# Squares of the hidden layer folded to one tile by VectorE before TensorE sums them, and the last unit's sums after its down products

## Chip, cores, metric

One Trainium2 chip, one of its cores. The metric is the device time of one execution in microseconds (us); a comparison is made between runs of the two kernels on the same chip. The kernel before takes 1067.99 us, the median of three runs (1066.66 to 1070.09).

## What is computed

A transformer block over 16 batches of 256 tokens, width 256, in fp32: an attention part with 16 heads of 128, and a feed-forward part whose weights are first made ternary by groups of 64. The change touches the feed-forward part and its normalisation alone:

```python
h = jax.nn.silu(gate) * up                                   # hidden, 1024 wide
inv = jax.lax.rsqrt(jnp.mean(h * h, axis=-1, keepdims=True) + eps)
y = jnp.einsum('bsh,dh->bsd', h * inv, wq_p)                 # down product
x = x + _layernorm(y, axis=-1)
```

The kernel does not scale `h` by `inv`. A layernorm follows, so it takes the down product of the plain `h` (called z), and puts the mean of the squares into the layernorm's epsilon: z_floor = sum(h*h) * 1e-5/1024 + 1e-5*eps, one number a token. So the row sums of `h*h` are needed when z is normalised, not earlier.

## The kernel before, in words

Two phases follow each other, the attention over 128 steps and then the feed-forward over 16 **units** u, one a batch; the first units' work begins while the last attention steps drain. Everything of a unit lies in SBUF. Its hidden layer of 1024 x 256 tokens is held turned, as 8 tiles of 128 x 256, and worked in 4 **chunks** c of two tiles (FC = 2), so one VectorE or ScalarE instruction handles 128x512.

Every engine runs its own instruction list, written out by hand in its `step(u0, s)`; only semaphores tie them. `FLAG` says how many steps behind a stage stands: statistics and turn of the input two and one units ahead of the up products, the sums, down product and z one step behind them. Per unit:

- TensorE (`step`, L1021): `up` 0, `up` 1 of unit u (16 matmuls a chunk, `xt_hi`/`xt_lo` are the halves of the input), `down` of unit u-1 (L1000, 32 matmuls into `Z_BANK`), the sums of unit u-1 (`sum_tiles`, L990: a matmul with a column of ones for each token tile and each of the tiles given to it), `up` 2, `turn_x2` of unit u+1, `up` 3.
- ScalarE (`step`, from L1274): `norm_z` (L1262), then `activate` c (silu, L1231), `high_hidden` c (the fp32r high half of h, L1238), `norm_x2` (L1254), `square_hidden` c (L1245) and `split_x2` (L1271); the last square of a unit is its last instruction in a step but for what follows in the next step.
- VectorE (`step`, from L1669): `multiply` c (L1608: silu times up, one operand from PSUM), `add_squares` 2 and `sum_squares` of the unit before (L1615, L1621), `stats_x2` (L1628, L1631), `stats_z` with `sum_floor` (L1655, L1637, L1660), `split_x2` (L1665), `add_squares` 0 (L1615).
- GpSimd (`step`, from L689): `split_hidden` c (the low half of h, L644), `invert_x2` (from L651), `add_x` (the residual, L677), `invert_z` (from L665).

The squares of a unit are 8 tiles. Before, `add_squares` 0 adds tiles 2, 3 to 0, 1; `add_squares` 2 adds 6, 7 to 4, 5; `sum_squares` adds 4, 5 to 0, 1; two tiles remain, and TensorE sums them with 2 x 2 matmuls. For the last unit only `add_squares` 0 is done, and TensorE sums the six other tiles with 2 x 6 matmuls, ahead of its last down chunk.

A name in the trace is that of the memory it lies in: `wo_hi`, `wo_lo` are the halves of h (the attention's weights are no longer needed), `wq_hi`, `wq_lo` the up and down weights, `arena` holds the hidden layer, its squares and all small vectors. A fp32 matmul with `ones` leaves two records in the trace.

Of the kernel before, what the change touches and what calls it, by code (L numbers as in the profile page):

```python
# [25 lines left out]
ALU = mybir.AluOpType  # L26
AX = mybir.AxisListType

P = 128
# [40 lines left out]
FC = 2  # L70
# [13 lines left out]
def sandwich_kernel(nc, x, wq, wkv, wkvh, wg, wout, wgu, wproj, rope, out):  # L84
    ctx = ExitStack()
    with ctx:
# [3 lines left out]
        def sem(name):  # L90
            return ctx.enter_context(nc.semaphore(name))
# [38 lines left out]
        def carve(*shape):  # L130
# [154 lines left out]
                                     "lo_done"))  # L285
        gate_ready, up_ready, gate_silu, h_ready, h_squared, ht_hi_done, ht_lo_done = (
            sem(k) for k in ("gate_ready", "up_ready", "gate_silu", "h_ready", "h_squared", "ht_hi_done", "ht_lo_done"))
        h_added, h_summed, sum_ready, z_floored, z_ready = (
            sem(k) for k in ("h_added", "h_summed", "sum_ready", "z_floored", "z_ready"))
        z_stats, z_aggr, z_eps, z_neg, z_inv, z_biased, z_norm, res_done = (  # L290
            sem(k) for k in ("z_stats", "z_aggr", "z_eps", "z_neg", "z_inv", "z_biased", "z_norm", "res_done"))
        tile_done = sem("tile_done")
# [4 lines left out]
        def at_least(eng, s, value):  # L297

            if not (isinstance(value, int) and value <= 0):
                eng.wait_ge(s, value)  # L300
# [58 lines left out]
        def last_unit(u):  # L359

            return isinstance(u, int) and u == BATCH - 1
# [388 lines left out]
        def _(pe):  # L750
# [238 lines left out]
                                                   x2_rows(u, i)[:, t, k * P:(k + 1) * P], ident[:, :])  # L989
                last.then_inc(x2_turned, 1)  # L990

            def sum_tiles(u, i, tiles):

                at_least(pe, z_floored, u)
                for t in range(NT):
                    for f in tiles:
                        last = nc.tensor.matmul(O_BANK[:, t:t + 1], squares[i][:, f, t * P:(t + 1) * P], ones[:, :],  # L997
                                                start=t == 0 and f == 0, stop=f == tiles[-1], skip_group_check=True)
                last.then_inc(sum_ready, 1)

            def down(u, i):

                for c in range(FT // FC):
                    if last_unit(u) and c == FT // FC - 1:
                        pe.wait_ge(h_added, u * 2 + 1)
                        pe.wait_ge(h_squared, (u + 1) * (FT // FC))
                        sum_tiles(u, i, [*range(FC), *range(2 * FC, FT)])
                    pe.wait_ge(ht_lo_done, u * (FT // FC) + (c + 1))
                    if c == 0:
                        if isinstance(u, int) and u == 1:  # L1010
                            pe.wait_ge(y_copied, STEPS)
                        at_least(pe, z_norm, (u - 1) * NT)
                    for t in range(NT):
                        parts = [(f, part[i]) for f in range(c * FC, (c + 1) * FC) for part in (ht_hi, ht_lo)]
                        for n, (f, part) in enumerate(parts):

                            last = nc.tensor.matmul(Z_BANK[i][:, t * E:(t + 1) * E], part[:, f, t * P:(t + 1) * P],  # L1017
                                                    wpr_t[:, f, :], start=c == 0 and t == 0 and n == 0, stop=f == FT - 1,
                                                    skip_group_check=True)
                last.then_inc(z_ready, 1)  # L1020

            def step(u0, s):
                at = unit_at(u0, s, FLAG["up"])
                if at and at[0] > 0:
                    up(*at, 0)
                at = unit_at(u0, s, FLAG["up"])
                if at:
                    up(*at, 1)
                at = unit_at(u0, s, FLAG["down"])
                if at:  # L1030
                    u, i = at
                    down(u, i)
                    if not last_unit(u):
                        pe.wait_ge(h_summed, u + 1)
                        sum_tiles(u, i, range(FC))
                at = unit_at(u0, s, FLAG["up"])
                if at:
                    up(*at, 2)
                at = unit_at(u0, s, FLAG["turn"])
                if at and at[0] > 0:  # L1040
                    turn_x2(*at)
                at = unit_at(u0, s, FLAG["up"])
                if at:
                    up(*at, 3)
# [320 lines left out]
        def _(dve):  # L1365
# [251 lines left out]
            def sum_squares(u, i):  # L1617

                a, b = (squares[i][:, k * FC:(k + 1) * FC, :] for k in (0, 2))
                dve.wait_ge(h_added, u * 2 + 2)  # L1620
                nc.vector.tensor_tensor(a, a, b, ALU.add).then_inc(h_summed, 1)  # L1621

            def stats_x2(u):
# [9 lines left out]
            def sum_floor(u, i):  # L1633

                dve.wait_ge(sum_ready, u + 1)
                at_least(dve, z_eps, u - 1)
                nc.vector.tensor_scalar(z_floor[i], O_BANK[:, 0:NT], LN_EPS / FF, LN_EPS * RMS_EPS, ALU.mult, ALU.add)\  # L1637
                    .then_inc(z_floored, 1)
# [8 lines left out]

            def stats_z(u, i):

                if last_unit(u):  # L1650
                    sum_floor(u, i)
                dve.wait_ge(z_ready, u + 1)
                at_least(dve, z_biased, u)
                for t in range(NT):
                    nc.vector.bn_stats(z_stat[:, t, :], Z_BANK[i][:, t * E:(t + 1) * E]).then_inc(z_stats, 1)  # L1655
                if not last_unit(u):
                    sum_floor(u, i)
                dve.wait_ge(z_stats, u * NT + NT)
                for t in range(NT):
                    nc.vector.bn_aggr(z_agg[:, t, :], z_stat[:, t, :]).then_inc(z_aggr, 2)  # L1660

            def split_x2(u, i):

# [3 lines left out]
                    .then_inc(x2_lo_done, 1)  # L1667

            def step(u0, s):  # L1669
                at = unit_at(u0, s, FLAG["up"])  # L1670
                if at and at[0] > 0:
                    multiply(*at, 0)
                at = unit_at(u0, s, FLAG["out"])
                if at and last_unit(at[0]):
                    for t in range(NT):
                        add_x(*at, t)
                at = unit_at(u0, s, FLAG["sum"])
                if at and not last_unit(at[0]):
                    add_squares(*at, 2)
                    sum_squares(*at)  # L1680
                at = unit_at(u0, s, FLAG["stats"])
                if at and at[0] > 0:
                    stats_x2(at[0])
                at = unit_at(u0, s, FLAG["up"])
                if at:
                    multiply(*at, 1)
                at = unit_at(u0, s, FLAG["z"])
                if at:
                    stats_z(*at)
                at = unit_at(u0, s, FLAG["up"])  # L1690
                if at:
                    multiply(*at, 2)
                at = unit_at(u0, s, FLAG["turn"])
                if at and at[0] > 0:
                    split_x2(*at)
                at = unit_at(u0, s, FLAG["up"])
                if at:
                    add_squares(*at, 0)
                    multiply(*at, 3)
# [136 lines left out]
```

## Time and profile before

| | |
|---|---|
| median of three runs | 1067.99 us |
| the profiled execution, its own time | 1069.97 us |
| span of its trace | 1068.2 us |
| TensorE busy | 1045.1 us (98%) |
| GpSimd busy | 932.6 us (87%) |
| ScalarE busy | 861.3 us (81%) |
| VectorE busy | 812.7 us (76%) |
| granted TensorE clock | 0.993 of full |
| feed-forward phase | about 856 us to the end |

The time of an execution is its span and some 2 us around it. Busy time is that of the records; matmuls overlap, so a busy TensorE isn't one at its peak. Each row of a timeline has a start and a duration in us, then engine, line, operation, tiles (out<-in), and in brackets the idle time before it with what ended that.

### The profile page before, as it was taken

The numbers are of one execution on the slowest core, as the hardware profiler recorded it, in microseconds if no ns is written. First come the engines' busy times: TensorE is split into PE (matmuls) and PEld (weight loads), VectorE is DVE, ScalarE is ACT, GpSimd is POOL, SyncE is SP. The second block draws the span as 40 slices with busy tenths as digits, with TensorE's granted clock in tenths as the row PEclk, the third lists the DMA queues.
The fourth block names the chain that finished last, engine by engine and source line by source line (L and its number), as shares of the span: only waits on it lengthen the run. The fifth ranks groups of instructions, "written<-read, shape, count | busy, mean of one in ns | idle before, by whom it ended". The sixth has DMA issues, their size and how long they took to land.

```text
span 1068.2 us, 25271 instructions
## 1 busy us (share of the span) xinstructions
PE 1045.1 (98%) x7978; PEld 1002.8 (94%) x7978; DVE 812.7 (76%) x2804; ACT 861.3 (81%) x2386; POOL 932.6 (87%) x928
## 2 busy tenths in 40 slices
PE   7899999999999999999999999999999999999997
PEld 6789999999999999999999999999999899999997
DVE  5777888878887888888788878886777656666653
ACT  4788888888898889888988898888888766666674
POOL 4688999999999999999999999999899658777785
PEclk8999999999999999999999999999999999999999
DMA  8451111112111211221121121111120000000001
GB/s 264 173 169 31 51 55 54 45 50 61 41 41 56 66 41 32 62 69 41 48 64 42 40 61 51 50 41 62 51 90 21 2 1 21 21 21 20 22 21 41
DMA packets 35125, 58.58 MB, mean 55 GB/s; under 512 B 3136, under 2 KB 16000, under 8 KB 34688
## 3 DMA queue, kind: packets, MB, share of 16 engines
q1 hardware_dynamic: 34992, 56.96, 17.1%
q8 instruction: 64, 1.05, 0.4%
q14 instruction: 69, 0.57, 0.2%
HBM read 50.92 MB, written 9.18 MB: 56 GB/s over the span
## 4 chain that ended last, share of the span: by engine, by line
POOL 61%; PE 20%; issue 15%; DVE 1%; ACT 1%; DMA 1%; POOLq 1%; ACTq 0%; DVEq 0%
POOL arena L595 15%; POOL arena L616 14%; POOL arena L627 14%; POOL arena L605 13%; PE psum L975 11%; PE psum L1017 5%; PE psum L997 1%; POOL arena L553 1%; POOL arena L577 1%; PE psum L755 1%; POOL X L586 1%; PE psum L988 1%; DMA arena<-kh_rows 0%; POOL arena L561 0%; POOLq L300 0%
## 5 line engine op out<-in xcount | busy, mean ns | idle before, releaser
L627 POOL TENSOR_TENSOR arena<-arena 128x768 f32<-128x768 f32 x128 | 196.1, 1532 | 17.5 <-DVE arena L1503 17.2
L605 POOL TENSOR_TENSOR arena<-arena 128x512 f32<-128x512 f32 x128 | 173.7, 1357 | 10.0
L595 POOL TENSOR_TENSOR arena<-arena,tables 128x512 f32<-128x512 f32 x128 | 166.7, 1302 | 16.3 <-ACT arena L1167 14.8
L1516 DVE SCALAR_TENSOR_TENSOR pt_split<-psum,vh_col,pt_split 128x256 fp32r<-128x256 f32 (+1 forms) x512 | 176.9, 406 | 2.7 <-ACT pt_split L1197 2.7
L616 POOL TENSOR_TENSOR arena<-arena 128x512 f32<-128x512 f32 x128 | 164.0, 1281 | 3.7 <-ACT arena L1141 3.1
L887 PE MATMUL psum<-arena 128*128 128x256 f32 x512 | 154.6, 384 | 3.3 <-POOL arena L605 3.1
L1178 ACT ACTIVATE arena<-arena 128x256 f32<-128x256 f32 x256 | 128.4, 502 | 32.0 <-DVE arena L1493 25.6
L755 PE MATMUL psum<-wo_hi,o_hi 128*128 128x256 f32 x512 | 152.7, 298 | 0.0
L755 PE MATMUL psum<-xt_hi,wq_hi 128*128 128x256 f32 x512 | 146.8, 287 | 0.0
L755 PE MATMUL psum<-xt_lo,wq_hi 128*128 128x256 f32 x512 | 145.3, 284 | 0.0
L755 PE MATMUL psum<-xt_hi,wq_lo 128*128 128x256 f32 x512 | 145.2, 284 | 0.0
L755 PE MATMUL psum<-wo_hi,o_lo 128*128 128x256 f32 x512 | 144.3, 282 | 0.0
L755 PE MATMUL psum<-wo_lo,o_hi 128*128 128x256 f32 x512 | 143.7, 281 | 0.0
L755 PE MATMUL psum<-pt_split,vals_hi 128*128 128x512 f32 (+1 forms) x512 | 142.0, 358 | 1.1 <-DVE wo_lo L1377 0.8
L975 PE MATMUL psum<-xt_hi,wq_hi 128*128 128x256 f32 x512 | 128.4, 290 | 0.8 <-DVE xt_lo L1665 0.8
L975 PE MATMUL psum<-xt_lo,wq_hi 128*128 128x256 f32 x512 | 124.7, 281 | 0.0
L1196 ACT ACTIVATE pt_split<-psum,vh_col 128x256 fp32r<-128x256 f32 x256 | 120.9, 472 | 0.1
L1166 ACT ACTIVATE arena<-psum 64x512 f32<-64x512 f32 x128 | 76.1, 595 | 53.6 <-DVE arena L1478 53.3
L1525 DVE TENSOR_TENSOR o_lo<-psum,o_hi 128x512 fp32r<-128x512 f32 x128 | 87.3, 682 | 33.5 <-ACT o_hi L1206 31.7
L889 PEld LDWEIGHTS psum<-arena 128*128 128x128 f32 x512 | 98.0, 191 | 13.7
L644 POOL TENSOR_TENSOR wo_lo<-arena,wo_hi 128x512 fp32r<-128x512 f32 x64 | 88.8, 1396 | 22.9 <-ACT wo_hi L1238 22.7
L1491 DVE CUSTOM_DVE_ANT_0 arena<-psum,mask 128x256 f32<-128x256 f32 x256 | 106.9, 417 | 1.1 <-issue 1.1
(185 smaller groups left out, 3448.4 us busy)
## 6 DMA issues: line engine op xcount, KB each, us to landing
arena<-kh_rows SPq DMA_DIRECT2D x127, 256.0 KB, 3.3
out<-spare SPq DMA_DIRECT2D x15, 256.0 KB, 2.1
arena<-w_rows SPq DMA_DIRECT2D x6, 512.0 KB, 4.7
X<-L_attn_Wout SPq DMA_DIRECT2D x1, 2048.0 KB, 14.7
X<-L_attn_x SPq DMA_DIRECT2D x1, 2048.0 KB, 13.6
arena<-L_attn_Wq SPq DMA_DIRECT2D x1, 1536.0 KB, 10.4
X<-L_attn_x SPq DMA_DIRECT2D x1, 1536.0 KB, 10.5
w_rows<-L_ffn_w_gate_up SPq DMA_DIRECT2D x3, 512.0 KB, 9.0
```

What stands on the lines that cost most here:

```text
L595: nc.gpsimd.tensor_tensor(swap, swap, spread, ALU.mult).then_inc(q_sined, 1)
L605: nc.gpsimd.tensor_tensor(q_rot[p % 2], q_cos[p % 2], q_swap[p % 2], ALU.add).then_inc(q_roped, 1)
L616: nc.gpsimd.tensor_tensor(k_head[p % 2], keys[par].unsqueeze(1).to_broadcast([P, HP, N]), kh_all[p % 4], ALU.mult).then_inc(k_scaled, 1)
L627: nc.gpsimd.tensor_tensor(tb, tb, r.unsqueeze(3).to_broadcast([P, HP, 3, P]), ALU.mult).then_inc(p_ready, 1)
L755: last = nc.tensor.matmul(o, a, b, start=start and i == 0, stop=stop and i == len(passes) - 1, skip_group_check=skip)
L887: nc.tensor.matmul(sj[:, 0:2 * P], q[:, j, P:N], kt[:, j, :], start=True, stop=True, skip_group_check=True)
L889: nc.tensor.matmul(sj[:, 2 * P:3 * P], q[:, j, 0:P], kt[:, j, 0:P], start=False, stop=True, skip_group_check=True).then_inc(s_ready, 1)
L975: last = nc.tensor.matmul(bank[c % 2 * 2 + half][:, j * N:(j + 1) * N], wgu_t[:, k, col:col + P], part[:, k, :], start=n == 0 and j == 0, ...
L1178: nc.scalar.activation(tb[:, j, 0:2 * P], tb[:, j, 0:2 * P], ACT.Exp, scale=-1.0, bias=nmax[p % 4][:, 2 * j:2 * j + 1], accum_out=rsum[p % ...
L1196: nc.scalar.activation(pt_hi[p % 2][:, j * N:(j + 1) * N], b[:, 0:N], ACT.Copy, scale=vh[:, 0, h:h + 1])
L1491: nc.vector.tensor_tensor_reduce(tb[:, j, 0:2 * P], S_BANK[j][:, 0:2 * P], mask[:, :], -1.0, -MASKED, ALU.add, ALU.min, nmax[p % 4][:, 2 * ...
L1516: last = nc.vector.scalar_tensor_tensor(pt_lo[p % 2][:, o], b[:, i], vh[:, t, h:h + 1], pt_hi[p % 2][:, o].bitcast(F32), ALU.mult, ALU.sub ...
```

## The change

`sum_squares` gets a second instruction: after two tiles remain, one is added to the other (128x256), and it waits for the first by a new semaphore, `h_halved`. TensorE sums the one remaining tile, with two matmuls. The last unit is treated like the others: all three kinds of add on VectorE, and two matmuls after its whole down product. On VectorE `add_squares` 2 and `sum_squares` of the unit before now stand at the head of the step, ahead of `multiply` 0, and `sum_floor` stands behind the aggregates of `stats_z` (in the last unit it stood ahead of `stats_z`).

```diff
@@ -285,8 +285,8 @@
                                      "lo_done"))
         gate_ready, up_ready, gate_silu, h_ready, h_squared, ht_hi_done, ht_lo_done = (
             sem(k) for k in ("gate_ready", "up_ready", "gate_silu", "h_ready", "h_squared", "ht_hi_done", "ht_lo_done"))
-        h_added, h_summed, sum_ready, z_floored, z_ready = (
-            sem(k) for k in ("h_added", "h_summed", "sum_ready", "z_floored", "z_ready"))
+        h_added, h_halved, h_summed, sum_ready, z_floored, z_ready = (
+            sem(k) for k in ("h_added", "h_halved", "h_summed", "sum_ready", "z_floored", "z_ready"))
         z_stats, z_aggr, z_eps, z_neg, z_inv, z_biased, z_norm, res_done = (
             sem(k) for k in ("z_stats", "z_aggr", "z_eps", "z_neg", "z_inv", "z_biased", "z_norm", "res_done"))
         tile_done = sem("tile_done")
@@ -989,22 +989,18 @@
                                                    x2_rows(u, i)[:, t, k * P:(k + 1) * P], ident[:, :])
                 last.then_inc(x2_turned, 1)
 
-            def sum_tiles(u, i, tiles):
-
+            def sum_tiles(u, i):
+
+                pe.wait_ge(h_summed, u + 1)
                 at_least(pe, z_floored, u)
                 for t in range(NT):
-                    for f in tiles:
-                        last = nc.tensor.matmul(O_BANK[:, t:t + 1], squares[i][:, f, t * P:(t + 1) * P], ones[:, :],
-                                                start=t == 0 and f == 0, stop=f == tiles[-1], skip_group_check=True)
+                    last = nc.tensor.matmul(O_BANK[:, t:t + 1], squares[i][:, 0, t * P:(t + 1) * P], ones[:, :],
+                                            start=t == 0, stop=True, skip_group_check=True)
                 last.then_inc(sum_ready, 1)
 
             def down(u, i):
 
                 for c in range(FT // FC):
-                    if last_unit(u) and c == FT // FC - 1:
-                        pe.wait_ge(h_added, u * 2 + 1)
-                        pe.wait_ge(h_squared, (u + 1) * (FT // FC))
-                        sum_tiles(u, i, [*range(FC), *range(2 * FC, FT)])
                     pe.wait_ge(ht_lo_done, u * (FT // FC) + (c + 1))
                     if c == 0:
                         if isinstance(u, int) and u == 1:
@@ -1030,9 +1026,7 @@
                 if at:
                     u, i = at
                     down(u, i)
-                    if not last_unit(u):
-                        pe.wait_ge(h_summed, u + 1)
-                        sum_tiles(u, i, range(FC))
+                    sum_tiles(u, i)
                 at = unit_at(u0, s, FLAG["up"])
                 if at:
                     up(*at, 2)
@@ -1618,6 +1612,9 @@
 
                 a, b = (squares[i][:, k * FC:(k + 1) * FC, :] for k in (0, 2))
                 dve.wait_ge(h_added, u * 2 + 2)
+                nc.vector.tensor_tensor(a, a, b, ALU.add).then_inc(h_halved, 1)
+                a, b = (squares[i][:, k, :] for k in range(FC))
+                dve.wait_ge(h_halved, u + 1)
                 nc.vector.tensor_tensor(a, a, b, ALU.add).then_inc(h_summed, 1)
 
             def stats_x2(u):
@@ -1647,17 +1644,14 @@
 
             def stats_z(u, i):
 
-                if last_unit(u):
-                    sum_floor(u, i)
                 dve.wait_ge(z_ready, u + 1)
                 at_least(dve, z_biased, u)
                 for t in range(NT):
                     nc.vector.bn_stats(z_stat[:, t, :], Z_BANK[i][:, t * E:(t + 1) * E]).then_inc(z_stats, 1)
-                if not last_unit(u):
-                    sum_floor(u, i)
                 dve.wait_ge(z_stats, u * NT + NT)
                 for t in range(NT):
                     nc.vector.bn_aggr(z_agg[:, t, :], z_stat[:, t, :]).then_inc(z_aggr, 2)
+                sum_floor(u, i)
 
             def split_x2(u, i):
 
@@ -1667,6 +1661,10 @@
                     .then_inc(x2_lo_done, 1)
 
             def step(u0, s):
+                at = unit_at(u0, s, FLAG["sum"])
+                if at:
+                    add_squares(*at, 2)
+                    sum_squares(*at)
                 at = unit_at(u0, s, FLAG["up"])
                 if at and at[0] > 0:
                     multiply(*at, 0)
@@ -1674,10 +1672,6 @@
                 if at and last_unit(at[0]):
                     for t in range(NT):
                         add_x(*at, t)
-                at = unit_at(u0, s, FLAG["sum"])
-                if at and not last_unit(at[0]):
-                    add_squares(*at, 2)
-                    sum_squares(*at)
                 at = unit_at(u0, s, FLAG["stats"])
                 if at and at[0] > 0:
                     stats_x2(at[0])
```

On VectorE, in a steady step, the rows from a unit's first `add_squares` to the aggregates of its z. Before (L1615 add, L1608 multiply, L1621 `sum_squares`, L1628 and L1631 `stats_x2`, L1655 and L1660 `stats_z`, L1637 `sum_floor`; of the two L1608 the second is `multiply` 0 of the next unit):

```order
L1615 TENSOR_TENSOR arena<-arena 128x512
L1608 TENSOR_TENSOR arena<-arena,psum 128x512 x2
L1615 TENSOR_TENSOR arena<-arena 128x512
L1621 TENSOR_TENSOR arena<-arena 128x512
L1628 BN_STATS arena<-X 128x6 x2
L1631 BN_AGGR arena<-arena 128x2 x2
L1608 TENSOR_TENSOR arena<-arena,psum 128x512
L1655 BN_STATS arena<-psum 128x6 x2
L1637 TENSOR_SCALAR arena<-psum 128x2
L1660 BN_AGGR arena<-arena 128x2 x2
```

In the changed kernel (L1609 add, L1602 multiply, L1615 `sum_squares`, L1618 its new second add, L1625 and L1628 `stats_x2`, L1650 and L1653 `stats_z`, L1634 `sum_floor`):

```order
L1609 TENSOR_TENSOR arena<-arena 128x512
L1602 TENSOR_TENSOR arena<-arena,psum 128x512
L1609 TENSOR_TENSOR arena<-arena 128x512
L1615 TENSOR_TENSOR arena<-arena 128x512
L1618 TENSOR_TENSOR arena<-arena 128x256
L1602 TENSOR_TENSOR arena<-arena,psum 128x512
L1625 BN_STATS arena<-X 128x6 x2
L1628 BN_AGGR arena<-arena 128x2 x2
L1602 TENSOR_TENSOR arena<-arena,psum 128x512
L1650 BN_STATS arena<-psum 128x6 x2
L1653 BN_AGGR arena<-arena 128x2 x2
L1634 TENSOR_SCALAR arena<-psum 128x2
```

`multiply` 0 of the next unit moved from ahead of the second add to behind three adds, and `sum_floor` from between the z statistics to behind them.

On TensorE, around the last unit's sums (L1017, and L1013 in the changed kernel, are the down product, L997 the sums). Before, the sums and what stands on both sides of them:

```order
L1017 MATMUL psum<-wq_lo,wo_hi 128x256
L1017 MATMUL psum<-wq_lo,wo_lo 128x256
L997 MATMUL psum<-ones,arena 128x1 x12
L1017 MATMUL psum<-wq_lo,wo_hi 128x256
L1017 MATMUL psum<-wq_lo,wo_lo 128x256
```

In the changed kernel, the end of the list:

```order
L1013 MATMUL psum<-wq_lo,wo_hi 128x256
L1013 MATMUL psum<-wq_lo,wo_lo 128x256
L1013 MATMUL psum<-wq_lo,wo_hi 128x256
L1013 MATMUL psum<-wq_lo,wo_lo 128x256
L997 MATMUL psum<-ones,arena 128x1 x2
L86 UNCONDITIONAL_BRANCH
```

Twelve matmuls ahead of the last eight down products became two behind them.

## Rows read from the trace of the kernel before

**Rows 1.** the page, part 1: busy us and share of the span, instructions

```profile
PE 1045.1 (98%) x7978; PEld 1002.8 (94%) x7978; DVE 812.7 (76%) x2804; ACT 861.3 (81%) x2386; POOL 932.6 (87%) x928
```

**Rows 2.** chain that ended last, 1030 us to the end: start, us, what

```profile
1050.61 0.79 PE psum L997 x8
...
1058.21 2.59 PE psum L997 x24
...
1063.13 0.19 POOL arena L665
```

**Rows 3.** waits from 850 us on: who for whom, us in total, times, longest

```profile
PEld psum L975 <- DVE xt_lo L1665: 3.1, 12, 0.5
```

**Rows 4.** timeline of VectorE, 974 to 990 us: start, us, engine, line, operation

```profile
976.45 0.68 DVE L1665 TENSOR_TENSOR xt_lo<-psum,xt_hi 128x512 fp32r<-128x512 f32 x1
977.05 1.76 DVE L1615 TENSOR_TENSOR arena<-arena 128x512 f32<-128x512 f32 x1
978.73 0.67 DVE L1608 TENSOR_TENSOR arena<-arena,psum 128x512 f32<-128x512 f32 x1
982.02 0.69 DVE L1608 TENSOR_TENSOR arena<-arena,psum 128x512 f32<-128x512 f32 x1 [2.61 <-ACT arena L1231]
982.62 0.68 DVE L1615 TENSOR_TENSOR arena<-arena 128x512 f32<-128x512 f32 x1
983.34 0.69 DVE L1621 TENSOR_TENSOR arena<-arena 128x512 f32<-128x512 f32 x1
...
985.03 0.69 DVE L1608 TENSOR_TENSOR arena<-arena,psum 128x512 f32<-128x512 f32 x1
...
989.53 0.68 DVE L1665 TENSOR_TENSOR xt_lo<-psum,xt_hi 128x512 fp32r<-128x512 f32 x1
```

**Rows 5.** timeline of ScalarE, 974 to 990 us

```profile
979.98 0.61 ACT L1245 ACTIVATE arena<-arena 128x512 f32<-128x512 f32 x1
...
981.40 0.59 ACT L1231 ACTIVATE arena<-psum 128x512 f32<-128x512 f32 x1
982.74 0.63 ACT L1238 ACTIVATE wo_hi<-arena 128x512 fp32r<-128x512 f32 x1 [0.75 <-DVE arena L1608]
983.28 0.58 ACT L1231 ACTIVATE arena<-psum 128x512 f32<-128x512 f32 x1
...
986.28 1.08 ACT L1254 ACTIVATE arena<-X,arena 128x256 f32<-128x256 f32 x2
```

**Rows 6.** timeline of GpSimd, 974 to 990 us

```profile
976.98 1.28 POOL L677 TENSOR_TENSOR spare<-arena,X 128x512 f32<-128x512 f32 x1
978.22 0.64 POOL L665 TENSOR_TENSOR arena<-arena 128x2 f32<-128x2 f32 x1
...
979.95 2.55 POOL L644 TENSOR_TENSOR wo_lo<-arena,wo_hi 128x512 fp32r<-128x512 f32 x2
983.45 1.75 POOL L644 TENSOR_TENSOR wo_lo<-arena,wo_hi 128x512 fp32r<-128x512 f32 x1 [0.95 <-ACT wo_hi L1238]
```

**Rows 7.** timeline of VectorE, the end of the kernel

```profile
1060.82 0.16 DVE L1637 TENSOR_SCALAR arena<-psum 128x2 f32<-128x2 f32 x1 [4.70 <-PE psum L997]
...
1065.08 0.88 DVE L1645 TENSOR_TENSOR spare<-arena,X 128x256 f32<-128x256 f32 x2 [2.09 <-ACT arena L1262]
```

**Rows 8.** timeline of VectorE, 853 to 885 us

```profile
870.93 1.79 DVE L1615 TENSOR_TENSOR arena<-arena 128x512 f32<-128x512 f32 x1
872.65 0.67 DVE L1608 TENSOR_TENSOR arena<-arena,psum 128x512 f32<-128x512 f32 x1
876.42 0.69 DVE L1608 TENSOR_TENSOR arena<-arena,psum 128x512 f32<-128x512 f32 x1 [3.10 <-ACT arena L1231]
...
879.44 0.69 DVE L1608 TENSOR_TENSOR arena<-arena,psum 128x512 f32<-128x512 f32 x1
```

**Rows 9.** timeline of GpSimd, 853 to 885 us

```profile
870.89 1.29 POOL L644 TENSOR_TENSOR wo_lo<-arena,wo_hi 128x512 fp32r<-128x512 f32 x1 [0.64 <-ACT wo_hi L1238]
```

**Rows 10.** timeline of GpSimd, 1055 to 1059 us

```profile
1056.87 1.30 POOL L644 TENSOR_TENSOR wo_lo<-arena,wo_hi 128x512 fp32r<-128x512 f32 x1 [0.62 <-ACT wo_hi L1238]
```

## The prediction

> **What bounds the kernel now.** I read the page first. TensorE is busy for 1045.1 of 1068.2 us [rows 1], and each feed-forward unit gives it eight records of row sums, 0.79 us in the chain [rows 2]. That reading alone says: halve them and win. The second view is the waits from 850 us on. TensorE does wait there, for the low half of the next unit's input, 12 times for 3.1 us, 0.26 us each [rows 3]; so once a unit TensorE stands at the end of somebody else's chain. The third view, one steady step on VectorE, GpSimd and ScalarE, shows that chain closed into a ring:
>
> - VectorE's `split_x2` from 976.45, first `add_squares` from 977.05 (it takes 1.76 us), `multiply` 3 from 978.73 [rows 4];
> - ScalarE's last square, 979.98 to 980.59, then `norm_z`, `activate` 0 from 981.40 [rows 5];
> - `multiply` 0 from 982.02, second `add_squares`, `sum_squares`, `stats_x2`, `multiply` 1 from 985.03 [rows 4];
> - ScalarE's `norm_x2` of the next unit from 986.28, the squares and `activate` 2 behind it [rows 5], and VectorE's `split_x2` again at 989.53: 13.08 us after the first [rows 4].
>
> No link of the ring has slack, except that `activate` 1 is over at 983.86, 1.17 us before the `multiply` that reads it: VectorE is busy with adds and statistics. TensorE alone would need 13.08 - 0.26 = 12.8 us. What counts is therefore when `multiply` 1 runs.
>
> **The port, which sets the durations.** The first `add_squares` takes 1.76 us, the second, of the same shape, 0.68 [rows 4]. The first starts 0.07 us after GpSimd's `add_x` (976.98 to 978.26) and ends 0.55 us after it; GpSimd's next, tiny instruction takes 0.64 us [rows 6] where it takes 0.19 at the end of the kernel [rows 2]. The other way round, `split_hidden` 0 starts at 983.45 under `sum_squares`, takes 1.75 us in place of 1.28 and ends 1.17 us after VectorE's 984.03 [rows 4, 6]. So an add of two SBUF tensors and a GpSimd instruction exclude each other; the waiting one goes next, even where the other engine has more work queued. `multiply`, which reads one operand from PSUM, overlaps GpSimd from 982.02 at its usual 0.69. The Trainium skill (SBUF — State Buffer, "Who interferes with whom") says that a VectorE instruction with two SBUF inputs contends with a GpSimd one that reads SBUF, and the later blocks fully: by that rule the trace agrees, and it speaks against moving such adds under GpSimd's long instructions.
>
> **The change part by part.**
>
> 1. TensorE: two matmuls a unit go, half of the eight records of 0.79 us [rows 2]: -0.40 us of its work. Worth nothing while the ring is slower.
>
> 2. VectorE gets one add of 128x256. Its price: the final residual adds, 128x256 of two SBUF inputs, take 0.88 for two overlapped, some 0.42 each [rows 7]; the bounds are 0.16 (the small floor instruction in the same rows) and 0.69 (the 512-column form). I take 0.42, nearest in shape.
>
> 3. The order: all three adds now stand ahead of `multiply` 0, behind ScalarE's last square (980.59). VectorE was idle there, from 979.4 to 982.02. With the port free, the adds would run 980.65 to 982.4 and `multiply` 0 would be 0.3 us late, `multiply` 1 about 1 us early. But GpSimd runs `split_hidden` 2 and 3 back to back from 979.95 to 982.50 [rows 6]. Laid out with the two offsets above: `split_hidden` 2 ends 981.23, the second `add_squares` 981.23 + 0.55 = 981.78; GpSimd waits for it and ends `split_hidden` 3 at 981.78 + 1.17 = 982.95. `sum_squares` must wait for the add's semaphore, so GpSimd is next in line: the sum ends at 982.95 + 0.55 = 983.50, the new add at 983.96, `multiply` 0 starts about 983.88: **1.86 us late**.
>
> 4. What is queued behind it: on ScalarE `high_hidden` 0 starts 0.72 after `multiply` 0, `activate` 1 another 0.54, and takes 0.58 [rows 5]; with 0.07 of semaphore `multiply` 1 starts 1.91 us after `multiply` 0, at 985.79 in place of 985.03. The statistics (about 1.1 us) fit in between. **The ring becomes 0.76 us longer per unit**, and everything from `norm_x2` to the next `add_squares` keeps its relative place, the 0.07 us by which GpSimd's `add_x` is ahead too. Bounds: -0.24 (VectorE keeps the port, below) and +0.9 (if the sum and the new add each pay 0.07 more in handing over). `split_hidden` 0 gets out from under the sum, which saves GpSimd 0.45 us that nobody waits for. TensorE: the last down chunk starts near 983.8 and has its low half at 982.95; the sums need `h_summed` at 983.96, TensorE comes to them after 984.5. Both are covered by the down products; without that cover the sums would cost up to 0.4.
>
> 5. Moving `sum_floor` behind the aggregates puts 0.14 us later on a result that GpSimd takes up several us later: nothing.
>
> 6. Entry. In unit 1 the first `add_squares` (870.93) is held by `split_hidden` 2 [rows 8, 9], which started 0.04 us before. TensorE is the bound there, and is 0.40 us ahead after the first shorter sum, so the add starts near 870.5, ahead of `split_hidden` 2, and costs 0.7. `multiply` 3, then held by TensorE, comes at about 871.3 in place of 872.65. Only one `split_hidden` (about 872.75 to 874.05) stands in the way of the new adds: 874.6, 875.3, 875.75; `multiply` 0 at 875.7 (before 876.42), `multiply` 1 at 875.7 + 1.91 = 877.6 (before 879.44): -1.8 us. Bounds: -0.4 (TensorE's share alone) and -1.9.
>
> 7. The end. Twenty-four records of sums, 2.59 us, stood between unit 15's third and fourth down chunk [rows 2]. They go: the last chunk then starts when its low half is there; before, that was 1058.17 [rows 10], when TensorE had just begun the sums. The price is VectorE's three adds behind the last square and one `split_hidden`, about 0.5 us past the last down product, with `sum_floor` (0.16) at the end. So -2.6 from the sums; but only about 0.3 comes back, since the first add and most of its wait fall under the down products: -2.3. Bounds: 0 and -2.6.
>
> **The sum.** Twelve steps (`multiply` 1 of units 3 to 14) at +0.76 are +9.1; entry -1.8; end -2.3: **+5.0 us**. Against the profiled execution's 1069.97 us that is 1075.0; that execution lies 2 us over the median of the three runs, 1067.99, so I forecast **1073.0 us** for the median. A measurement of this kernel can tell about 0.3%, 3.2 us, from no change. The forecast's own range, 0.6 to 0.9 a step and 0 to -2.6 at the end, is 1070 to 1077.
>
> **The rivals.**
>
> *A: VectorE keeps the port between its dependent adds* (ends on the other side). The adds then end 981.78, 982.50 and 982.96, `multiply` 0 starts at 982.88, `multiply` 1 at 984.79, 0.24 us earlier than now. It decides if GpSimd's waiting instruction is not let in during the 0.04 us between an add and the next that waits for it (the gap between 983.30 and 983.34 in [rows 4]). Twelve times -0.24, -1.8 and -2.3 give -7.0: 1061. Against it: GpSimd leaves no longer gap between `add_x` and its next instruction, and VectorE got in. Chance 0.14.
>
> *B: the adds are not held up at all, TensorE is the bound.* The ring falls under TensorE's time, and a unit saves 0.26 + 0.40 us: 12 x 0.66 = 7.9, with 0.4 at entry and 2.3 at the end -10.6: 1057. Against it stands the 1.76 us add. For it: 98% busy on the page. Chance 0.07.
>
> *C: the places shift so that in half of the steps the first `add_squares` gets ahead of `add_x`.* It lost by 0.07 us [rows 4, 6]; ahead, it ends up to 1.1 us earlier. Half the steps at that gain are 12 x (0.76 - 0.55) = +2.5, so -1.6 in all: 1066.4. Both engines count from the same end of `norm_x2`, which speaks against a shift; for it there is only how small 0.07 us is. Chance 0.13.
>
> **How the numbers follow.** Forecast 0.66. Of it 0.05 falls under +3.2 us. Slower by over 0.3%: 0.61. Within: 0.05 + 0.12 of C = 0.17. Faster: A and B and the rest of C, 0.22. The range reaches from A's 1061 to the forecast's upper end 1077, and leaves out B and the tails, under 0.2.
>
> **What would show it.** In a steady step of the changed kernel: the second `add_squares` takes about 1.2 us, `sum_squares` 1.7, the new add 0.42; `split_hidden` 3 about 1.7; `multiply` 1 to `multiply` 1 is 13.8 us; TensorE waits about 1.3 us a unit, at the turn and for `split_x2`. At the end, the first down chunk to the last instruction is 2 us shorter. The forecast is wrong if `sum_squares` takes 0.69 us right behind the add (A), if no add is over 0.8 us (B), or if the first `add_squares` comes back to 0.7 (C). It would be wrong in size if `multiply` 0 started under 1.5 us later after the last square than I say, 3.3 us.

## The result, and the profile after

The changed kernel takes 1073.18 us, the median of 12 runs (1071.71 to 1076.28); the kernel before, measured beside it, 1068.08 us (12 runs, 1066.66 to 1070.52). The ratio is 1.0044 (95% interval 1.0034 to 1.0053): slower by 0.4%, clear of the spread, 5.1 us at the medians.

The page's first part, against [rows 1]: TensorE's busy time fell by 8.8 us and VectorE's rose by 27.2, although the work added to VectorE is 16 adds of 0.42 us and the last unit's two. Nearly all of the rest is time in which its adds stood still: an instruction that is held up has a longer record, not an idle time before it.

```profile
PE 1036.3 (97%) x7898; PEld 991.8 (93%) x7898; DVE 839.9 (78%) x2822; ACT 861.8 (81%) x2386; POOL 933.6 (87%) x928
```

A steady step on VectorE (start, us, engine, line, operation; the line numbers moved by 6: L1602 `multiply`, L1609 `add_squares`, L1615 `sum_squares`, L1618 the new add, L1659 `split_x2`):

```profile
977.00 0.68 DVE L1659 TENSOR_TENSOR xt_lo<-psum,xt_hi 128x512 fp32r<-128x512 f32 x1
977.60 1.75 DVE L1609 TENSOR_TENSOR arena<-arena 128x512 f32<-128x512 f32 x1
979.27 0.67 DVE L1602 TENSOR_TENSOR arena<-arena,psum 128x512 f32<-128x512 f32 x1
981.17 1.17 DVE L1609 TENSOR_TENSOR arena<-arena 128x512 f32<-128x512 f32 x1 [1.22 <-ACT arena L1239]
982.37 1.67 DVE L1615 TENSOR_TENSOR arena<-arena 128x512 f32<-128x512 f32 x1
984.07 0.42 DVE L1618 TENSOR_TENSOR arena<-arena 128x256 f32<-128x256 f32 x1
984.41 0.68 DVE L1602 TENSOR_TENSOR arena<-arena,psum 128x512 f32<-128x512 f32 x1
...
986.28 0.69 DVE L1602 TENSOR_TENSOR arena<-arena,psum 128x512 f32<-128x512 f32 x1 [0.17 <-ACT arena L1225]
...
990.77 0.68 DVE L1659 TENSOR_TENSOR xt_lo<-psum,xt_hi 128x512 fp32r<-128x512 f32 x1
```

and on GpSimd in the same step (L677 `add_x`, L644 `split_hidden`, the pair with 3.00 us being 2 and 3):

```profile
977.52 1.28 POOL L677 TENSOR_TENSOR spare<-arena,X 128x512 f32<-128x512 f32 x1
...
980.49 3.00 POOL L644 TENSOR_TENSOR wo_lo<-arena,wo_hi 128x512 fp32r<-128x512 f32 x2
985.84 1.29 POOL L644 TENSOR_TENSOR wo_lo<-arena,wo_hi 128x512 fp32r<-128x512 f32 x1 [2.35 <-ACT wo_hi L1232]
```

The second `add_squares` takes 1.17 us where [rows 4] have 0.68, `sum_squares` 1.67 where they have 0.69, and the pair of `split_hidden` 3.00 where [rows 6] have 2.55. `multiply` 0 starts 3.27 us after ScalarE's last square (which ends 981.14) where before it started 1.43 us after it (982.02 against 980.59): 1.84 us late. `multiply` 1 follows 1.87 us behind `multiply` 0. From `split_x2` to `split_x2` the step is 13.77 us, 0.69 longer than the 13.08 of [rows 4].

TensorE waits more. The waits between 930 and 1020 us, seven units, after:

```profile
PEld psum L988 <- ACT arena L1248: 6.0, 7, 0.9
PE psum L988 <- ACT arena L1248: 4.5, 7, 0.7
PEld psum L975 <- DVE xt_lo L1659: 3.4, 7, 0.5
PE psum L975 <- DVE xt_lo L1659: 1.9, 7, 0.3
```

That is 0.9 us a unit of idle matmul time (4.5 and 1.9 us in seven), 1.3 us for weight loads, where before the same window had 0.3 and 1.6 us in all.

**Where the 5 us are.** Each of the 16 units has one `split_x2`, and each has a row, so a profiled execution can be cut at them. I start at unit 1's; unit 0's lies 39.6 us ahead of it in both kernels, among the last attention steps. From unit 1's to the end of the span, the kernel before takes 211.3 us (856.87 to 1068.2) and the changed one 216.25 us (854.35 to 1070.6), 4.9 us more. The first two steps after that cut, 13.02 and 12.39 us where 13.46 and 13.60 stood, are the entry, 1.65 us gained. The next twelve, from unit 3's to unit 15's (879.76 to 1045.91), are 166.15 us against 157.76 (883.93 to 1041.69): 8.4 lost. The rest, 24.69 against 26.51, is the end: 1.8 gained.

The twelve are not all alike. Nine lost 0.68 to 0.74 us each. The first lost 0.42: its first `add_squares` took 1.47 us in the changed kernel and 1.74 before. One lost 0.38, because there the kernel before stood 0.33 us ahead of `multiply` 1 for a reason that the profile doesn't show. The last lost 1.21: it has no `stats_x2`, which made it the shortest before (12.59 us), but in the changed kernel it took 13.80 like the others.

### The profile page after: what moved, and what is told of

It is laid out like the page before. It is cut to its first block, busy times and chain, and to the rows that moved or that the text cites. A ratio compares the mean times of both kernels' runs of the same rounds, so it can differ in the third digit from the quotient of the medians.

```text
span 1070.6 us, 25129 instructions
## 1 busy us (share of the span) xinstructions
PE 1036.3 (97%) x7898; PEld 991.8 (93%) x7898; DVE 839.9 (78%) x2822; ACT 861.8 (81%) x2386; POOL 933.6 (87%) x928
## 4 chain that ended last, share of the span: by engine, by line
POOL 58%; issue 16%; PE 16%; DVE 5%; ACT 3%; DMA 1%; POOLq 0%; ACTq 0%; DVEq 0%
POOL arena L595 15%; POOL arena L616 14%; POOL arena L627 13%; POOL arena L605 12%; PE psum L975 8%; PE psum L1013 4%; PE psum L755 2%; DVE arena L1602 1%; ACT arena L1248 1%; POOL arena L553 1%; POOL arena L577 1%; PE psum L988 1%; DVE arena L1609 1%; ACT arena L1225 1%; POOL X L586 1%
## 5 line engine op out<-in xcount | busy, mean ns | idle before, releaser
L644 POOL TENSOR_TENSOR wo_lo<-arena,wo_hi 128x512 fp32r<-128x512 f32 x64 | 88.3, 1388 | 37.1 <-ACT wo_hi L1232 36.9
```

## Experiments

The theory: VectorE, ScalarE and GpSimd form a ring that is the bound of a step, and what lengthens it is that VectorE's adds of two SBUF tensors and GpSimd's instructions exclude each other. The rivals: the new add costs by its duration alone; the order costs nothing; TensorE is the bound. In the table, "step" is the usual distance of two `split_x2` between 930 and 1000 us, "last 12" the time from unit 3's `split_x2` to unit 15's, "end" from there to the end of the span. "Fold" is short for the new add of 128x256 with the two matmuls that it saves.

| kernel | ratio to before (95%) | median us | step | last 12 | end |
|---|---|---|---|---|---|
| before | 1 | 1068.1 to 1069.1 | 13.07 | 157.8 | 26.5 |
| changed | 1.0044 (1.0034 to 1.0053) | 1073.2 | 13.78 | 166.2 | 24.7 |
| changed, run again | 1.0045 (1.0028 to 1.0061) | 1073.5 | 13.78 | 166.1 | 24.7 |
| fold, old order | 1.0111 (1.0095 to 1.0127) | 1081.3 | 14.51 | 173.0 | 25.1 |
| new order, no fold | 0.9983 (0.9974 to 0.9993) | 1067.5 | 13.32 | 159.8 | 25.0 |
| last unit alone | 0.9987 (0.9977 to 0.9997) | 1067.2 | 13.08 | 157.9 | 25.2 |
| TensorE's matmuls given back | 1.0065 (1.0050 to 1.0081) | 1075.8 | 13.78 | 166.4 | 26.0 |
| reductions for the wide adds | 0.9998 (0.9987 to 1.0009) | 1068.3 | 13.47 | 162.0 | 24.2 |
| adds behind `multiply` 1, fold | 0.9899 (0.9879 to 0.9918) | 1056.8 | 12.34 | 149.2 | 25.7 |
| the same, no fold | 0.9936 (0.9919 to 0.9954) | 1062.9 | 12.79 | 153.5 | 25.2 |

**Fold in the old order.** The three adds go back behind `multiply` 0.

```diff
             def step(u0, s):
-                at = unit_at(u0, s, FLAG["sum"])
-                if at:
-                    add_squares(*at, 2)
-                    sum_squares(*at)
                 at = unit_at(u0, s, FLAG["up"])
                 if at and at[0] > 0:
                     multiply(*at, 0)
...
+                at = unit_at(u0, s, FLAG["sum"])
+                if at:
+                    add_squares(*at, 2)
+                    sum_squares(*at)
                 at = unit_at(u0, s, FLAG["stats"])
```

> The change with its three adds put back behind multiply 0 (the order before), fold and last unit kept. Theory (the port decides): split_hidden 0 of GpSimd starts under sum_squares and is next in line when that ends, so the new 0.42 us add waits for it and ends about 1.4 us after sum_squares; multiply 1 then starts about 1.4 us later than before in every steady step, the step is 14.4 us, the kernel 12 x 1.4 - 2 (end) - 1 (entry) = about +14 us, 1082. Rival (an add costs its 0.42 us, the port matters nowhere else than at the first add): +0.46 us a step, the kernel +2 to +3 us, 1070.5.

Measured: 1081.3 us, a step of 14.51. VectorE, then GpSimd:

```profile
989.45 0.69 DVE L1609 TENSOR_TENSOR arena<-arena 128x512 f32<-128x512 f32 x1
990.17 0.69 DVE L1615 TENSOR_TENSOR arena<-arena 128x512 f32<-128x512 f32 x1
990.90 1.40 DVE L1618 TENSOR_TENSOR arena<-arena 128x256 f32<-128x256 f32 x1
992.23 0.74 DVE L1625 BATCH_NORM_STATS2 arena<-X 128x6 f32<-128x256 f32 x2
```

```profile
990.28 1.74 POOL L644 TENSOR_TENSOR wo_lo<-arena,wo_hi 128x512 fp32r<-128x512 f32 x1 [0.94 <-ACT wo_hi L1232]
```

Neither wide add is held; the new one, of 256 columns, takes 1.40 us, because `split_hidden` 0 came at 990.28 under `sum_squares`, waited, and went in between the two dependent adds. This is the hand-over on which rival A rested, in a place of its own: GpSimd gets the port. Fold and last unit together, in the old order, cost 12.2 us against the kernel before. The right partner for the fold alone is the kernel "last unit alone" below, which differs from this one by the fold only: the fold costs 14.0 us at the medians, 1.43 us a step (14.51 against 13.08). The new order takes back half of that, 0.73 us a step.

**New order without the fold.** `sum_squares` ends with the wide add, and TensorE sums two tiles.

```diff
-                nc.vector.tensor_tensor(a, a, b, ALU.add).then_inc(h_halved, 1)
-                a, b = (squares[i][:, k, :] for k in range(FC))
-                dve.wait_ge(h_halved, u + 1)
                 nc.vector.tensor_tensor(a, a, b, ALU.add).then_inc(h_summed, 1)
```

> The new order without the new add: TensorE sums two tiles again (four matmuls a unit). Theory: without the 0.42 us add and its 0.04 of semaphore, multiply 0 comes 1.4 us late against before instead of 1.86, multiply 1 +0.30 us, a step 13.4 us; entry -1, end -2: about +0.6 us, 1068.7. Rival (the new add is the whole loss, the order costs nothing): a step of 12.9 us (TensorE's), the kernel 4 to 6 us faster than before.

Measured: 1067.5 us, a step of 13.32. The wide adds take 1.16 and 1.67 us as in the changed kernel. So the order alone costs 0.25 us a step, and the fold on top of it 0.46, its 0.42 us and a semaphore. The total came out better than expected, 1.8 us under the kernel before by the ratio where +0.6 was expected: over the last 12 steps the order cost 2.0 us, the expectation has 3.6.

**The last unit alone**, in the kernel before. In the last unit VectorE now does all three wide adds, as in the others, where it did only `add_squares` 0, and TensorE does four matmuls behind the down product in place of twelve inside it. `sum_floor` stands behind the aggregates, as in the changed kernel.

```diff
             def down(u, i):
...
-                    if last_unit(u) and c == FT // FC - 1:
-                        pe.wait_ge(h_added, u * 2 + 1)
-                        pe.wait_ge(h_squared, (u + 1) * (FT // FC))
-                        sum_tiles(u, i, [*range(FC), *range(2 * FC, FT)])
...
                     down(u, i)
-                    if not last_unit(u):
-                        pe.wait_ge(h_summed, u + 1)
-                        sum_tiles(u, i, range(FC))
+                    sum_tiles(u, i)
...
-                if at and not last_unit(at[0]):
+                if at:
                     add_squares(*at, 2)
                     sum_squares(*at)
```

> The kernel before, with its last unit alone handled like the others (three adds on VectorE, four matmuls behind the whole down product). Theory: steady steps unchanged at 13.07 us, the 2.59 us of sums go from the end and some 0.6 us come back by the wait for the squares' sum: 1.9 us faster, 1066.2. Rival (VectorE's adds and GpSimd's residual in the same port give it all back): no change.

Measured: 1067.2 us, a gain of 1.4 us by the ratio (0.3 to 2.5); in the profile the end is 1.35 us shorter (25.16 against 26.51), the steady step is as before (13.08) and the last 12 take 157.9 us against 157.8. The rival has part of it: at the end the adds are held here too (1.37 and 1.65 us, not 0.69 each), but that doesn't give it all back.

**TensorE's work given back** to the changed kernel.

```diff
                 for t in range(NT):
-                    last = nc.tensor.matmul(O_BANK[:, t:t + 1], squares[i][:, 0, t * P:(t + 1) * P], ones[:, :],
-                                            start=t == 0, stop=True, skip_group_check=True)
+                    for r in range(2):
+                        last = nc.tensor.matmul(O_BANK[:, t:t + 1], squares[i][:, 0, t * P:(t + 1) * P], ones[:, :],
+                                                start=t == 0 and r == 0, stop=r == 1, skip_group_check=True)
```

> The changed kernel with each of its two sum matmuls done twice, so TensorE has its 0.40 us a unit again (the row sums come out doubled). Theory (the ring of VectorE, ScalarE and GpSimd is the bound, TensorE waits 1.3 us a unit): no change against the changed kernel, 1073 (at most +0.2). Rival (TensorE is the bound, 97% busy): +0.40 us a unit, 1079.

Measured: 1.0065, against 1.0044 for the changed kernel; the intervals touch, the ratios are 2.2 us apart. Neither number was expected. The profile separates them: the step is 13.78 us, the same to 0.01, so in the steady part TensorE's 0.4 us are free; they are taken out of its wait at the turn, which falls from 4.5 to 1.4 us in the seven units above. But the first three steps are 0.45, 0.67 and 0.29 us longer than in the changed kernel, and the end 1.3 us: there TensorE's work counts, and the theory's "at most +0.2" had left both out. At the entry it counts twice, because with the matmuls back the first `add_squares` comes behind `split_hidden` 2 again and takes 1.80 us (at 867.16) in place of 0.68. The end on VectorE, `sum_floor` (L1635) waiting for the doubled sums:

```profile
1065.70 0.25 DVE L1654 BATCH_NORM_AGGREGATE arena<-arena 128x2 f32<-128x6 f32 x2
1066.63 0.16 DVE L1635 TENSOR_SCALAR arena<-psum 128x2 f32<-128x2 f32 x1 [0.67 <-PE psum L998]
```

**Reductions in place of the wide adds**, one SBUF input each.

```diff
-                nc.vector.tensor_tensor(a, a, b, ALU.add).then_inc(h_added, 1)
+                if c:
+                    dve.wait_ge(h_added, u * 2 + 1)
+                    nc.vector.tensor_reduce(squares[i][:, FC:2 * FC, :], pairs(squares[i][:, 2 * FC:4 * FC, :]), AX.X, ALU.add)\
+                        .then_inc(h_added, 1)
+                else:
+                    nc.vector.tensor_tensor(a, a, b, ALU.add).then_inc(h_added, 1)
...
-                nc.vector.tensor_tensor(a, a, b, ALU.add).then_inc(h_halved, 1)
+                nc.vector.tensor_reduce(squares[i][:, 2 * FC:3 * FC, :], pairs(squares[i][:, 0:2 * FC, :]), AX.X, ALU.add)\
+                    .then_inc(h_halved, 1)
```

> The changed kernel with its second add_squares and its sum_squares written as a pairwise tensor_reduce: one SBUF input each, twice the elements read, so about 1.2 us each where a free add takes 0.68. Theory (port): nothing holds them, nor do they hold split_hidden 3; 1.2 + 1.2 + 0.42 against 1.17 + 1.67 + 0.42, multiply 0 comes about 0.4 us earlier than in the changed kernel, a step 13.35 us, the kernel about 5 us faster than the changed one, 1068. Rival (the adds are slow for another reason, such as GpSimd's traffic in SBUF slowing every VectorE instruction, or the semaphores): the reductions take 1.7 us and more, the kernel is 6 us or more slower than the changed one.

Measured: 1068.3 us, a step of 13.47. VectorE, then GpSimd:

```profile
978.10 1.25 DVE L1615 TENSOR_REDUCE arena<-arena 128x512 f32<-128x1024 f32 x1 [1.22 <-ACT arena L1239]
979.39 1.26 DVE L1623 TENSOR_REDUCE arena<-arena 128x512 f32<-128x1024 f32 x1
980.69 0.43 DVE L1627 TENSOR_TENSOR arena<-arena 128x256 f32<-128x256 f32 x1
981.03 0.68 DVE L1602 TENSOR_TENSOR arena<-arena,psum 128x512 f32<-128x512 f32 x1
```

```profile
977.42 2.55 POOL L644 TENSOR_TENSOR wo_lo<-arena,wo_hi 128x512 fp32r<-128x512 f32 x2
```

A reduction reads the same 1024 elements a partition as an add of two 512-column tiles, but all through one input (the expectation's "twice the elements" is true of that input alone), and takes 1.25 us where a free add takes 0.68. It takes that everywhere: all 32 in the kernel lie between 1.25 and 1.27 us, whatever GpSimd does meanwhile. Here they run under `split_hidden` 2 and 3, which keep their 2.55 us. `multiply` 0 starts 981.03, 0.3 us sooner behind the square than in the changed kernel. That the form with the longer free time finishes sooner is what a port that is waited for explains, and general slowness of SBUF doesn't. The Trainium skill (SBUF — State Buffer, "Who interferes with whom") has it that a VectorE instruction with at most one SBUF input, outside the two-port modes, does not contend with GpSimd; for these reductions the trace agrees.

**The adds behind `multiply` 1, TensorE's sums behind `up` 2**, with the fold and without it. The adds are taken away from the head of the step. The two moves were not tried one by one.

```diff
                     multiply(*at, 1)
+                at = unit_at(u0, s, FLAG["sum"])
+                if at:
+                    add_squares(*at, 2)
+                    sum_squares(*at)
                 at = unit_at(u0, s, FLAG["z"])
...
                     down(u, i)
-                    sum_tiles(u, i)
                 at = unit_at(u0, s, FLAG["up"])
                 if at:
                     up(*at, 2)
+                at = unit_at(u0, s, FLAG["down"])
+                if at:
+                    sum_tiles(*at)
```

> The changed kernel with its three adds behind multiply 1 and TensorE's sums behind up 2. Theory: multiply 1 waits for activate 1 alone, 1.1 us earlier than before, the ring falls to about 12.0 us and TensorE's 12.47 us become the step: 0.6 us less than before in 12 steps, -7; entry and end -2 to -3: about 1058.5. Rival (the adds now hold stats_z, sum_floor and multiply 2 back, or the sums stall TensorE): a step over 13 us, 1066 or more.

> The same without the new add, four sum matmuls a unit. Theory: TensorE's 12.87 us are the step, -0.2 us in 12 steps, entry and end -2 to -3: about 1063, 4 to 5 us slower than with the fold. Rival (the fold buys nothing there either): the same time as with the fold.

Measured: 1056.8 us with the fold, 1.0% under the kernel before and, by the ratios, 1.4% under the changed one; 1062.9 without it (1058.5 and 1063 were expected). VectorE, from `multiply` 1, then the same kernel's busy times over 70 us (columns: PE, PEld, DVE, ACT, POOL busy with their counts, clock, DMA share, GB/s):

```profile
974.24 0.80 DVE L1611 TENSOR_TENSOR arena<-arena 128x512 f32<-128x512 f32 x1
975.07 0.69 DVE L1617 TENSOR_TENSOR arena<-arena 128x512 f32<-128x512 f32 x1
975.79 0.42 DVE L1620 TENSOR_TENSOR arena<-arena 128x256 f32<-128x256 f32 x1
...
978.33 0.16 DVE L1636 TENSOR_SCALAR arena<-psum 128x2 f32<-128x2 f32 x1 [1.08 <-PE psum L997]
```

```profile
940.00:1010.00 70.00, 70.00 (x592) 70.00 (x592) 43.87 (x101) 51.15 (x97) 52.40 (x75) 1.00 0.07 24
```

```profile
940.00:1010.00 70.00, 65.40 (x532) 63.31 (x531) 50.96 (x92) 45.72 (x88) 48.68 (x67) 1.00 0.06 20
```

The adds take 0.80, 0.69 and 0.42 us, in a stretch in which GpSimd has little to do; the first `add_squares`, no longer behind `add_x`, takes 0.71 us in these steps in place of 1.75. TensorE is busy for all 70.00 us where in the changed kernel (the second fence) it is for 65.40, and the step is TensorE's own 12.34 us. Here, and only here, the fold is worth what its matmuls cost: 0.45 us a step between the two variants.

## Why the prediction was right

1,073.0 us was forecast for the median, 1,073.18 measured; +5.0 us for the profiled pair, +4.9 found from unit 1's `split_x2` on. The mechanism, a ring whose adds are held by GpSimd, is the one measured. The agreement to 0.2 us is luck: the three parts were missed by -0.7, +0.15 and +0.5 us, which cancel. Point by point:

- **TensorE's share** (point 1): worth nothing in the steady step, shown by giving it back. The wait of about 1.3 us a unit is that of its weight loads (1.3); its matmuls wait 0.9. At the entry and the end it was worth something, 1.4 (the first three steps) and 1.3 us.
- **The new add** (2): 0.42 us, in the row as forecast.
- **The order and the port** (3): second `add_squares` 1.13 forecast and 1.17 measured; `sum_squares` some 1.68 and 1.67; `multiply` 0 late by 1.86 and 1.84. A side sum is off: with the port free the adds would end 982.5, not 982.4, and `multiply` 1 would be 0.7 us early, not about 1; nothing hangs on it.
- **The ring** (4): +0.76 forecast for each of twelve steps, +0.69 or so measured in a steady one (13.77 against 13.08). `multiply` 1 follows `multiply` 0 by 1.87 us, not 1.91: the 0.07 us put down for the semaphore measured 0.04. That the average of the twelve is 0.70 too is chance, since the steps with 0.42, 0.38 and 1.21 even out; the forecast has no term for the last of them. The lead of `add_x` over the first `add_squares` stayed (977.52 against 977.60 above), and that add took 1.75 to 1.77 us for units 4 to 14, so rival C didn't come about.
- **`sum_floor`** (5): nothing, as forecast; in the kernel with the last unit alone it is moved as well, and the step stays 13.08.
- **The entry** (6): -1.8 forecast, -1.65 found. The first `add_squares` was free there, 0.68 us, because TensorE was ahead, as forecast. With TensorE's matmuls given back it took 1.80 us and the two steps gained only 0.5, so that link is tested. The rows of the changed kernel:

```profile
867.98 0.68 DVE L1609 TENSOR_TENSOR arena<-arena 128x512 f32<-128x512 f32 x1
868.73 0.69 DVE L1602 TENSOR_TENSOR arena<-arena,psum 128x512 f32<-128x512 f32 x1
870.64 1.37 DVE L1609 TENSOR_TENSOR arena<-arena 128x512 f32<-128x512 f32 x1 [1.22 <-ACT arena L1239]
872.04 0.69 DVE L1615 TENSOR_TENSOR arena<-arena 128x512 f32<-128x512 f32 x1
...
873.11 0.68 DVE L1602 TENSOR_TENSOR arena<-arena,psum 128x512 f32<-128x512 f32 x1
```

  Before, that first add took 1.79 us [rows 8].
- **The end** (7): -2.3 forecast, -1.8 found, and the failed term is "about 0.3 comes back". From the end of the last down product (1061.84 before, 1062.95 after) to the end of the span it takes 6.36 us before and 7.65 after: 1.3 us come back. The last unit's down product, with the sums that stood in it, became 2.4 us shorter (2.6 forecast), and 0.7 us were gained ahead of it, which the forecast's end doesn't have; without that 0.7 it would have been -1.1. From the first down chunk to the last instruction it is 1.1 us shorter (13.02 to 11.91), not 2. The working had the adds meet one `split_hidden`; they met GpSimd's `add_x` of unit 14 as well, which stood behind it and went in between the first add and the sum:

```profile
1060.86 1.37 DVE L1609 TENSOR_TENSOR arena<-arena 128x512 f32<-128x512 f32 x1 [1.22 <-ACT arena L1239]
1062.26 1.65 DVE L1615 TENSOR_TENSOR arena<-arena 128x512 f32<-128x512 f32 x1
1063.95 0.42 DVE L1618 TENSOR_TENSOR arena<-arena 128x256 f32<-128x256 f32 x1
1064.29 0.76 DVE L1650 BATCH_NORM_STATS2 arena<-psum 128x6 f32<-128x256 f32 x2
```

```profile
1060.38 1.30 POOL L644 TENSOR_TENSOR wo_lo<-arena,wo_hi 128x512 fp32r<-128x512 f32 x1 [0.44 <-ACT wo_hi L1232]
1061.81 1.55 POOL L677 TENSOR_TENSOR spare<-arena,X 128x512 f32<-128x512 f32 x1
1065.53 0.19 POOL L665 TENSOR_TENSOR arena<-arena 128x2 f32<-128x2 f32 x1 [2.17 <-DVE arena L1634]
```

  `sum_squares` takes 1.65 us instead of 0.69, and z's statistics, whose last down product ends at 1062.95, wait for VectorE until 1064.29. This is the same hand-over as in the steady step; `add_x` was left out of the list of what GpSimd still had queued.
- **Rivals.** A (VectorE keeps the port between dependent adds) fell in all twelve steps, in each of which `sum_squares` took 1.67 us right behind the add, and in the 1.40 us add of the fold in the old order once more. B (TensorE bounds) fell by the unchanged step when TensorE got its work back. It was not foolish: once the ring is shorter, TensorE does bound, at 12.34 us.

## What to carry to other kernels

An engine that is 98% busy may still stand at the end of a ring of others: take one step and follow each engine's link until it closes, before paying for less work on the busiest. Adds of two SBUF tensors on VectorE are cheap beside an idle GpSimd (0.68 us here) and cost nearly a whole GpSimd instruction more beside a busy one (1.67 to 1.80), and of a chain of dependent ones each link can lose the port anew; so place them by GpSimd's list, or give them one input from PSUM or a reduction (`multiply`, with one operand in PSUM, and the reductions kept their time beside GpSimd here). Before adding work to an engine, ask which of its instructions the others wait for, and put the new work behind those: the same fold adds 1.43 us to a step in the old place (14.51 against 13.08) and 0.46 in the given one (13.78 against 13.32), and takes 0.45 off behind `multiply` 1 (12.34 against 12.79), where TensorE is the bound.

## What was not expected

The part that nobody touched varies more than the steady steps. Unit 1's `split_x2` came at 856.87 us before and 854.35 in the changed kernel, 854.56 in its second profile, 856.96 in the new order without the fold and 858.08 in the last variant. The three profiles over 856 have a first slice (one fortieth of the span) with a granted clock of 8 tenths, the other seven 9. From 13 to 27 us the granted clock was 0.76 of full before and 0.88 in the changed kernel. So the late start goes with TensorE's clock at the start. It need not be the program: runs of the kernel before on one chip reach from 1066.7 us at a mean clock of 0.997 to 1071.7 at 0.990. Steady steps, in contrast, repeat to 0.03 us but for the few named above. Comparing spans alone, the profiled pair would have shown +2.4 us, half of the loss.

One step, from unit 4's `split_x2` to unit 5's, is 1 us longer than its neighbours in both kernels (14.06 us before, 14.80 after), and for two different reasons. Before, ScalarE does the last two normalisations of the attention part in it, 1.08 us:

```profile
900.56 0.62 ACT L1245 ACTIVATE arena<-arena 128x512 f32<-128x512 f32 x1
901.08 1.08 ACT L1118 ACTIVATE arena<-arena 128x256 f32<-128x256 f32 x2
902.06 1.00 ACT L1262 ACTIVATE arena<-psum,arena 128x256 f32<-128x256 f32 x2
```

That step grows by 0.98 us, nearly all of it. So in the kernel before, ScalarE between its last square and `multiply` 0 is a link of the ring, which the prediction only inferred. In the changed kernel the same two normalisations are done, and cost nothing: `activate` 0 is over at 899.81, and `multiply` 0, behind the adds, starts at 901.73. What lengthens the step there is the port, a third time in a row. GpSimd has one more instruction queued behind `split_hidden` 3, the last residual of the attention part (L586), and it goes in between `sum_squares` and the new add:

```profile
898.69 1.67 DVE L1615 TENSOR_TENSOR arena<-arena 128x512 f32<-128x512 f32 x1
900.39 1.41 DVE L1618 TENSOR_TENSOR arena<-arena 128x256 f32<-128x256 f32 x1
```

```profile
896.81 3.00 POOL L644 TENSOR_TENSOR wo_lo<-arena,wo_hi 128x512 fp32r<-128x512 f32 x2
899.77 1.75 POOL L586 TENSOR_TENSOR X<-X,arena 128x512 f32<-128x512 f32 x1
```

The new add takes 1.41 us in place of 0.42, which is the 1.0 us by which this step is longer than the next. Without that add ("new order, no fold") the same step takes 13.32 us like its neighbours, so neither the normalisations nor L586 cost anything there. So the change moved the ring: it now runs through the adds, and ScalarE's `norm_z` and `activate` 0 have slack.
